# A mixture-of-experts and recurrence kernel: gathered rows as pairs of halves turned by DMA, x mixed before the projections of r and k

## The chip, the cores and the metric

The kernel runs on one core of a Trainium2 chip. Engines: PE (matmuls), DVE, ACT, POOL (here also the issuer of gathers and scatters) and SP (the issuer of all other DMAs). The metric is the device time of one execution in microseconds; the figure for a kernel is the median of its runs.

## The reference

x is 16 x 512 x 128. Its layer norm xn feeds two branches, and the output is x + s * silu(g):

- s is a linear recurrence (16 heads of 8). xx is xn shifted by one token less xn; `xr = xn + xx*maa_r`, `xk = xn + xx*maa_k`, `xv = xn + xx*maa_v`; r, k, v are their projections by 128 x 128 matrices plus a bias; a decayed state runs over the tokens; the result is projected by Wo.
- g is a mixture of experts: a softmax over 8 gates, the two best experts of each token, each expert `(silu(t@w1) * (t@w3)) @ w2` with 512 hidden units, and a shared expert of the same size; half the shared result plus half the weighted sum.

All products are made at nearly full precision: each operand is split in a high and a low half-precision part, and a product is three matmuls (high-high, high-low, low-high).

## The kernel before, in words

**Prologue (0 to some 40 us).** 16 batches of 512 rows are loaded (`rows`), normalised, transposed by PE (`pe_flip`) and kept as `xh` and `xl`, high and low halves with channels on partitions. SP writes the normalised float rows to `normed_rows` in HBM, one write a batch (`sp_normed`, L474), each after the batch's normalisation and independent of the others.

**Steps.** The experts run in 206 steps (`steps`, L310). A unit is 512 rows of the shared expert (16 units), 512 rows sorted for one expert (wide, 25 units) or 256 sorted rows (narrow, 21 units); wide and shared units have four steps, narrow ones two. A step is two up-projections (`pe_up`, L1534, six matmuls of 512 columns), SiLU on ACT (L781), a product on DVE (L1218), a split into halves (ACT L785; DVE L1222 or, in early steps, POOL L624), and, three steps later, the down-projection (`pe_down`, L1561). Steps 0 to 47 are twelve shared units; during them DVE computes the routing, ending in `source` and `dest` (rows to gather, places to scatter to) at step 40. Then come two narrow units, the wide ones and the other narrow ones, with the last four shared units between them.

**Weights.** Nine sets (shared, eight experts) pass through a staging buffer of two slots. SP issues the loads in its program order (`sp_weights`, L459): sets 0 and 1 ahead of the `sp_normed` writes, set k = 2 right behind them, the others in the steps. ACT makes the high half (`act_split_w`, L758, L766), DVE the low one (L1013), in fixed steps: set 2 in steps 8, 10 and 12. ACT, DVE, PE, POOL and SP each work strictly in program order.

**Sorted rows.** There are 71 blocks of 256 sorted rows. POOL (`pool_sorted`, L626) gathers a block by two indirect DMAs of 128 float rows into `srows` (ring of three), and scatters results (`pool_scatter`, L638) by two more; block q's gather stands ahead of block q - 7's scatter, in one fixed order. Before a block is used PE transposes it (`pe_sorted`, L1501, L1509, two transposes), ACT casts the high half (L777) and DVE subtracts for the low one (L1211), into `sx`, a ring of four blocks.

**r and k.** From step 75 on, every fourth step carries one of 32 parts (`part_at`, L418): 512 columns of r (the first 16 parts), then of k (the other 16). The mix with the shifted x is folded into the weights (`wph`, `wpl` hold them scaled by maa and by 1 - maa), so a part is six matmuls, three on x and three on the shifted x (`pe_part`, L1581, L1596). ACT adds the bias (L817), DVE makes the decayed copy (L1232), SP stores both to HBM (`sp_part`, L479). The weights of k, v and Wo are prepared on DVE in steps 72 to 90 (`LATE_STEP`).

**Attention stage.** After the last scatter, 16 units run the recurrence: loads of r, k, their decayed copies and the experts' rows, then matmuls, DVE and POOL work and the output.

SP's order around the change:

```
sp_start()
sp_weights(0)
sp_weights(1)
for b in range(nb):
    sp_normed(b)
k = 2
for i in range(NS):
    while k <= EXPERTS and SPLIT_AT[3 * k - 6] <= i:
        sp_weights(k)
```

Of the kernel before, what the change touches and what calls it, by code (L numbers as in the profile page):

```python
# [12 lines left out]
P = 128  # L13
# [12 lines left out]
UNIT = 256  # L26
# [43 lines left out]
def build(nc, nb, x, decay, per_head, maa, wT, bias, bias_rows, gateT, w1e, w3e, w2e, w1s, w3s, w2s, const, out):  # L70
# [12 lines left out]
    rows_in = nc.dram_tensor("normed_rows", (NTOK, P), F32, kind="Internal").ap()  # L83
# [5 lines left out]
    with ctx:  # L89
# [65 lines left out]
        NXB = 3  # L155
        srows = sb("srows", [P, NXB, TPU, P])
        RING = 4
        sx = sb("sx", [P, 2, RING, UNIT], F16)
        sxh, sxl = [sx[:, i, :, :] for i in range(2)]
# [27 lines left out]
        take = carve(sx[:, :, :, :].rearrange("p a b c -> p (a b c)").bitcast(F32))  # L187
# [33 lines left out]
        ws32r = early([P, 2, P])  # L221
# [6 lines left out]
        ws32 = late([P, 7, P])  # L228
        wph = sb("wph", [P, 7, P], F16)
        wpl = sb("wpl", [P, 7, P], F16)  # L230
# [16 lines left out]
        ypair = take([P, 2, TPU, P])  # L247

# [80 lines left out]
        def flips_at(i):  # L329

            v, j = steps[i]
            todo = blocks_of.get(v + 1, [])
            at = j - (2 if wide(v) else 0) if len(todo) == 1 else j // 2 if wide(v) and j % 2 == 0 else -1 if wide(v) else j
            return [todo[at]] if 0 <= at < len(todo) else []
# [79 lines left out]
        LATE_STEP = 72  # L414
        R_PARTS, PARTS = NA, 2 * NA
# [15 lines left out]
        SCATTER_LAG = 7  # L431

# [7 lines left out]
        def sync_program(e):  # L440
# [12 lines left out]
            def sp_late():  # L453
                nc.sync.wait_ge(sem["normed_out"], 16 * nb)
# [19 lines left out]
            def sp_normed(b):  # L474
                normed(nc.sync, b)
                nc.sync.dma_start(rows_in[b * SEQ:(b + 1) * SEQ, :].rearrange("(t p) d -> p t d", p=P),
                                  rows[:, b * TPS:(b + 1) * TPS, :]).then_inc(sem["normed_out"], 16)

            def sp_part(n):  # L479
                u = n % R_PARTS  # L480
                plain, decayed = (r_rows, rd_rows) if n < R_PARTS else (k_rows, kd_rows)
# [8 lines left out]
            def sp_r(u):  # L490
                if u == 0:
                    nc.sync.wait_ge(sem["w_lo"], 3 * (EXPERTS + 1))
                sp_stored(u)
# [12 lines left out]
            def sp_k(u):  # L506
# [4 lines left out]
                sp_stored(R_PARTS + u)  # L511
# [42 lines left out]
            for b in range(nb):  # L554
                sp_normed(b)
            k = 2
            for i in range(NS):
# [5 lines left out]
                n = part_at(i)  # L563
                if n is not None:
                    sp_part(n)
                if n == RRING + 1:
                    for u in range(RRING - 1):
                        sp_r(u)
                if n == R_PARTS + KRING + 1:
# [34 lines left out]
        def pool_program(e):  # L604
# [21 lines left out]
            def pool_sorted(q):  # L626
                if q == 0:
                    G.wait_ge(sem["normed_out"], 16 * nb)
                    G.wait_ge(sem["source"], 1)
                if q >= NXB:  # L630
                    G.wait_ge(sem["s_flipped"], q - NXB + 1)
                for t in range(TPU):
                    at = block_at[q] * TPU + t
                    G.indirect_dma_start(srows[:, q % NXB, t, :], None, rows_in,  # L634
# [12 lines left out]
            def pool_state0():  # L647
                G.wait_ge(sem["w_hi"], 3 * (EXPERTS + 1))
# [84 lines left out]
        def act_program(e):  # L733
# [24 lines left out]
            def act_split_w(k, part):  # L758
# [3 lines left out]
                if (e, part) == (FREE_EXPERTS, 0):  # L762
                    A.wait_ge(sem["decays"], 4)
                    A.wait_ge(sem["mixes"], 6)
# [7 lines left out]

            def act_sorted(q):
                if q == 0:
                    A.wait_ge(sem["dest"], 1)
                A.wait_ge(sem["s_flipped"], q + 1)
                A.copy(sxh[:, q % RING, :], psum[6][:, q % 2 * UNIT:(q % 2 + 1) * UNIT]).then_inc(sem["s_hi"], 1)  # L777
# [31 lines left out]
            def act_part(n):  # L809
                col = n // R_PARTS  # L810
# [6 lines left out]
                A.activation(rbuf[:, n % 2, :], psum[7], ACT.Identity, bias=brs[:, col:col + 1]).then_inc(sem["part_out"], 1)  # L817

# [81 lines left out]
            for i in range(NS + LAG):  # L900
                y = i - LAG if i >= LAG and last_step_of(i - LAG) else None
                if i < NS:
                    act_up(i)
                    for q in flips_at(i):
                        act_sorted(q)
# [4 lines left out]
                    filled = flips_at(i) or splits_of(i) or block_sets(i - 1)  # L910
                    if y is not None and not filled:
                        act_down(steps[y][0])
                    if part_at(i - 1) is not None:
                        act_part(part_at(i - 1))
                    act_split(i)
                    if y is not None and filled:
# [31 lines left out]
        def dve_program(e):  # L948
# [22 lines left out]
            def dve_r_weights(step):  # L971

                if step == 0:
# [4 lines left out]
                    V.tensor_scalar(ws32r[:, 0, :], w32r[:, :], omx[:, 0:1], SW, ALU.mult, ALU.mult).then_inc(sem["mixes"], 1)  # L978
                    V.tensor_scalar(ws32r[:, 1, :], w32r[:, :], mx[:, 0:1], SW, ALU.mult, ALU.mult).then_inc(sem["mixes"], 1)
                if step == 1:  # L980
                    V.wait_ge(sem["mixes"], 4)
                    V.tensor_copy(wph[:, 0:4:3, :], ws32r[:, :, :]).then_inc(sem["mixes"], 1)
                    V.wait_ge(sem["mixes"], 5)
                    V.tensor_tensor(wpl[:, 0:4:3, :], ws32r[:, :, :], wph[:, 0:4:3, :], ALU.subtract).then_inc(sem["mixes"], 1)
# [70 lines left out]
            def dve_fulls():  # L1055

                V.wait_ge(sem["scanned"], EXPERTS)
                V.wait_ge(sem["normed_out"], 16 * nb)
# [150 lines left out]
            def dve_sorted(q):  # L1209
                V.wait_ge(sem["s_hi"], q + 1)  # L1210
                V.tensor_tensor(sxl[:, q % RING, :], psum[6][:, q % 2 * UNIT:(q % 2 + 1) * UNIT], sxh[:, q % RING, :],  # L1211
                                ALU.subtract).then_inc(sem["s_lo"], 1)

# [10 lines left out]
            def dve_part(n):  # L1224
                w = wb if n < R_PARTS else wk
                V.wait_ge(sem["part_out"], n + 1)
                if n == 0:
                    V.wait_ge(sem["hot_used"], NHOTS)
                    V.wait_ge(sem["mixes"], 7)
# [560 lines left out]
```

## Time and profile before

| | |
|---|---|
| runs | 722.7, 721.18, 720.07 us; median 721.18 us |
| the profiled execution | span 719.3 us from its first to its last instruction; its own device time beside that is not given; the median of the runs is 1.9 us above the span |
| expert stage with sorted rows | first gather 154.67 us, last scatter 554.04 us |
| instructions | 22370; PE 8536 matmuls, DVE 1058, ACT 1008, POOL 519 |

A row of the timeline gives start and duration in us, engine, line, operation, output<-input; in brackets the idle time before it and what ended it. "xN" joins N instructions. The ends of PE's matmuls are modelled, so the pace of PE is read from the distance of starts. A row of the groups of instructions gives shapes, count, busy us and mean ns. DMA issues on SP carry the engine name SPq; landing is from issue to completion.

### The profile page before, as it was taken

The numbers are of one execution on the slowest core, as the hardware profiler recorded it, in microseconds if no ns is written. First come the engines' busy times: TensorE is split into PE (matmuls) and PEld (weight loads), VectorE is DVE, ScalarE is ACT, GpSimd is POOL, SyncE is SP. The second block draws the span as 40 slices with busy tenths as digits, with TensorE's granted clock in tenths as the row PEclk, the third lists the DMA queues.
The fourth block names the chain that finished last, engine by engine and source line by source line (L and its number), as shares of the span: only waits on it lengthen the run. The fifth ranks groups of instructions, "written<-read, shape, count | busy, mean of one in ns | idle before, by whom it ended". The sixth has DMA issues, their size and how long they took to land.

```text
span 719.3 us, 22370 instructions
## 1 busy us (share of the span) xinstructions
PE 654.1 (91%) x8536; PEld 452.1 (63%) x8536; DVE 555.4 (77%) x1058; ACT 494.9 (69%) x1008; POOL 478.9 (67%) x519
## 2 busy tenths in 40 slices
PE   2787897978999999999999999999997899999993
PEld 1544565646665665566666666878886676777772
DVE  5989986877667886667766676667664899999996
ACT  4864798857665656666666666666665788888872
POOL 4844321244777777777777777767778487888873
PEclk9999999999999999999999999999999999999997
DMA  9931111111111323433323334333362767777762
GB/s 243 299 95 45 45 61 46 45 51 36 48 49 49 108 91 108 137 108 108 110 92 109 106 106 139 110 101 108 97 103 93 237 179 230 216 229 222 233 176 59
DMA packets 88616, 86.75 MB, mean 121 GB/s; under 512 B 11394, under 2 KB 65284, under 8 KB 88516
## 3 DMA queue, kind: packets, MB, share of 16 engines
q1 hardware_dynamic: 79428, 66.70, 29.8%
q0 software_dynamic: 9088, 18.63, 9.6%
q8 instruction: 73, 1.20, 0.7%
q14 instruction: 27, 0.22, 0.1%
HBM read 50.82 MB, written 34.47 MB: 119 GB/s over the span
## 4 chain that ended last, share of the span: by engine, by line
PE 53%; DVE 13%; ACT 12%; POOL 11%; issue 7%; DMA 3%; SPq 0%; POOLq 0%; DVEq 0%; ACTq 0%
PE banks L1556 7%; PE banks L1558 7%; PE banks L1557 7%; PE banks L1596 5%; DVE hidden L1218 4%; POOL expert_rows L644 4%; PE banks L1576 4%; PE banks L1577 4%; PE banks L1575 4%; POOL srows L634 3%; ACT hidden L785 3%; PE banks L1621 3%; PE banks L1693 3%; PE banks L1672 3%; ACT rows L823 2%
## 5 line engine op out<-in xcount | busy, mean ns | idle before, releaser
L785 ACT CAST hidden<-hidden 128x512 f16<-128x512 f32 x206 | 127.1, 617 | 135.5 <-DVE hidden L1218 135.4
L634 POOL DMA_INDIRECT srows<-normed_rows,source x142 | 149.7, 1054 | 60.4 <-issue 40.2
L1222 DVE TENSOR_TENSOR hidden<-hidden 128x512 f16<-128x512 f32 x180 | 124.4, 691 | 83.9 <-ACT hidden L785 83.0
L1218 DVE TENSOR_TENSOR hidden<-hidden,banks 128x512 f32<-128x512 f32 x206 | 140.8, 684 | 44.0 <-ACT hidden L781 38.2
L1575 PE MATMUL banks<-wwords,hidden 128*128 (+1 forms) x824 | 148.8, 219 | 1.5 <-DVE hidden L1222 1.1
L1576 PE MATMUL banks<-wwords,hidden 128*128 (+1 forms) x824 | 148.6, 219 | 0.0
L1577 PE MATMUL banks<-wwords,hidden 128*128 (+1 forms) x824 | 148.6, 219 | 0.0
L781 ACT ACTIVATE hidden<-banks 128x512 f32<-128x512 f32 x206 | 122.7, 596 | 28.1 <-PE banks L1558 27.8
L1556 PE MATMUL banks<-sx,wwords 128*128 128x512 f16 (+1 forms) x368 | 121.5, 330 | 3.2 <-DVE wwords L1013 2.7
L1558 PE MATMUL banks<-sx,wwords 128*128 128x512 f16 (+1 forms) x368 | 121.6, 330 | 0.0
L1557 PE MATMUL banks<-sx,wwords 128*128 128x512 f16 (+1 forms) x368 | 121.5, 330 | 0.0
L644 POOL DMA_INDIRECT expert_rows<-ybuf,dest x72 | 77.2, 1072 | 22.8 <-issue 19.8
L1575 PEld LDWEIGHTS banks<-wwords,hidden 128*128 128x128 f16 x824 | 80.6, 98 | 12.4 <-issue 2.0
L644 POOL DMA_INDIRECT expert_rows<-rows,dest x70 | 72.8, 1040 | 23.1 <-issue 20.1
L1576 PEld LDWEIGHTS banks<-wwords,hidden 128*128 128x128 f16 x824 | 80.6, 98 | 11.3
L624 POOL TENSOR_TENSOR hidden<-hidden 128x512 f16<-128x512 f32 x26 | 33.6, 1294 | 76.8 <-ACT hidden L785 76.8
L1303 DVE TENSOR_TENSOR wwords<-banks,wmat 128x1024 f32<-128x1024 f32 x64 | 75.3, 1217 | 10.9 <-PE banks L1672 10.5
L1577 PEld LDWEIGHTS banks<-wwords,hidden 128*128 128x128 f16 x824 | 80.6, 98 | 0.0
L1556 PE MATMUL banks<-xh,wwords 128*128 128x512 f16 x128 | 49.2, 385 | 19.1 <-DVE hidden L1218 18.7
L1321 DVE SCALAR_TENSOR_TENSOR hidden<-banks,cst,hidden 128x256 f32<-128x256 f32 x128 | 61.5, 481 | 3.8 <-ACT hidden L849 0.7
L1558 PEld LDWEIGHTS banks<-sx,wwords 128*128 x368 | 36.0, 98 | 25.6
L1557 PE MATMUL banks<-xl,wwords 128*128 128x512 f16 x128 | 49.0, 383 | 0.0
(218 smaller groups left out, 1429.7 us busy)
## 6 DMA issues: line engine op xcount, KB each, us to landing
rows<-x SPq DMA_DIRECT2D x32, 256.0 KB, 4.9
rows<-expert_rows SPq DMA_DIRECT2D x32, 256.0 KB, 3.6
normed_rows<-rows SPq DMA_DIRECT2D x16, 256.0 KB, 3.9
r_rows<-rows SPq DMA_DIRECT2D x16, 256.0 KB, 2.1
rd_rows<-rows SPq DMA_DIRECT2D x16, 256.0 KB, 2.2
stage<-r_rows SPq DMA_DIRECT2D x16, 256.0 KB, 4.0
k_rows<-rows SPq DMA_DIRECT2D x16, 256.0 KB, 2.2
kd_rows<-rows SPq DMA_DIRECT2D x16, 256.0 KB, 2.2
```

The costliest lines, as they stand in the source:

```text
L634: G.indirect_dma_start(srows[:, q % NXB, t, :], None, rows_in, bass.IndirectOffsetOnAxis(source[:, at:at + 1], 0)).then_inc(sem[f"s_in{q % ...
L644: G.indirect_dma_start(rows_out, bass.IndirectOffsetOnAxis(dest[:, at:at + 1], 0), ring_of(q)[:, t, :], None).then_inc(sem[f"y_stored{q % ...
L781: A.activation(sg[:, i % 2, :], psum[2 * (i % 2)][:, :], ACT.Silu, scale=1.0 / SW).then_inc(sem["silu"], 1)
L785: A.copy(guh[:, i % 4, :], gu[:, i % 2, :]).then_inc(sem["gu_hi"], 1)
L1218: V.tensor_tensor(gu[:, i % 2, :], sg[:, i % 2, :], psum[2 * (i % 2) + 1][:, :], ALU.mult).then_inc(sem["gated"], 1)
L1222: V.tensor_tensor(gul[:, i % 4, :], gu[:, i % 2, :], guh[:, i % 4, :], ALU.subtract).then_inc(sem["gu_lo"], 1)
L1556: T.matmul(o, a, mh, start=True, stop=False)
L1557: T.matmul(o, a, ml, start=False, stop=False)
L1558: k = T.matmul(o, b, mh, start=False, stop=True)
L1575: T.matmul(o, guh[:, i % 4, s], a, start=(j == 0 and n == 0), stop=False)
L1576: T.matmul(o, guh[:, i % 4, s], b, start=False, stop=False)
L1577: k = T.matmul(o, gul[:, i % 4, s], a, start=False, stop=last)
```

## The change

1. Rows for the gather are kept as pairs: `normed_rows` holds, per token, 128 high and 128 low halves (512 bytes as before). SP makes them by transposing `xh` and `xl` batch by batch with DMA transposes (two a batch, 128 x 512 halves each) into a buffer with two slots, and writes each slot out.
2. A gathered block is turned by one DMA transpose on SP (`sp_turn`) straight into `sx`; PE's transposes, ACT's cast and DVE's subtraction for blocks go. `srows` becomes a ring of five. SP's turns stand in its program order at the first step of the unit before.
3. r and k take turns (part n is r for even n, k for odd n). x is mixed ahead: sum of the halves (DVE, one in two parts, four steps ahead), scaled shifted part (ACT, four steps ahead), mix (DVE, three ahead), high half (ACT, two ahead), low half (DVE, two ahead); a part is then three matmuls. The stores follow three steps after.
4. Weights of k, v and Wo are prepared from step 50 on; r and k weights are no longer scaled by maa.

```diff
+        NXB = 5
+        srows = sb("srows", [P, NXB, TPU, 2, P], F16)
+        PAIRS = NXB * TPU // TPS
...
-            def sp_normed(b):
-                normed(nc.sync, b)
+            def sp_pair(b):
+                s = b % PAIRS
+                nc.sync.wait_ge(sem["x_lo"], b + 1)
+                if b >= PAIRS:
+                    nc.sync.wait_ge(sem[f"pair_out{s}"], 16 * (b // PAIRS))
+                for h, half in enumerate((xh, xl)):
+                    nc.sync.dma_start(pairs[:, s, :, h, :], half[:, b * XS + 2:(b + 1) * XS],
+                                      transpose=True).then_inc(sem[f"pair_in{s}"], 16)
+
+            def sp_pair_out(b):
+                s = b % PAIRS
+                nc.sync.wait_ge(sem[f"pair_in{s}"], 32 * (b // PAIRS + 1))
                 nc.sync.dma_start(rows_in[b * SEQ:(b + 1) * SEQ, :].rearrange("(t p) d -> p t d", p=P),
-                                  rows[:, b * TPS:(b + 1) * TPS, :]).then_inc(sem["normed_out"], 16)
+                                  pairs[:, s, :, :, :].rearrange("p t h d -> p t (h d)")).then_inc(sem[f"pair_out{s}"], 16)
+
+            def sp_turn(q):
+                nc.sync.wait_ge(sem[f"s_in{q % NXB}"], 16 * TPU * (q // NXB + 1))
+                if q >= RING:
+                    nc.sync.wait_ge(sem["up"], last_up[unit_of[q - RING]])
+                nc.sync.dma_start(sx[:, q % RING, :, :, :].rearrange("p t h d -> p (t h) d"),
+                                  srows[:, q % NXB, :, :, :].rearrange("p t h d -> p (t h d)"),
+                                  transpose=True).then_inc(sem[f"turned{q % RING}"], 16)
...
-            for b in range(nb):
-                sp_normed(b)
+            for b in range(nb + 1):
+                if b < nb:
+                    sp_pair(b)
+                if b >= 1:
+                    sp_pair_out(b - 1)
...
+                for q in turned_at(i):
+                    sp_turn(q)
+                n = part_at(i - 3)
...
                 if q >= NXB:
-                    G.wait_ge(sem["s_flipped"], q - NXB + 1)
+                    turned(G, q - NXB)
...
+            def dve_mix(n):
+                proj = n % 2
+                V.wait_ge(sem["mix_prev"], n + 1)
+                m = mixed[:, :].rearrange("p (b i) -> p b i", b=4)
+                V.scalar_tensor_tensor(m, xsum[:, :, 1:P + 1], omx[:, proj:proj + 1], m, ALU.mult, ALU.add).then_inc(sem["mixed"], 1)
...
             def pe_part(n):
+                T.matmul(psum[7], wph[:, proj, :], mix_hi[:, :], start=True, stop=False)
+                T.matmul(psum[7], wph[:, proj, :], mix_lo[:, :], start=False, stop=False)
+                T.matmul(psum[7], wpl[:, proj, :], mix_hi[:, :], start=False, stop=True).then_inc(sem["part"], 1)
```

## Rows read from the trace of the kernel before

**Rows 1.** The page, part 1: busy us, share of the span, instructions.
```profile
PE 654.1 (91%) x8536; PEld 452.1 (63%) x8536; DVE 555.4 (77%) x1058; ACT 494.9 (69%) x1008; POOL 478.9 (67%) x519
```

**Rows 2.** Windows of 50 us: PE, PEld, DVE, ACT, POOL busy (count), clock, DMA.
```profile
335.00:385.00 50.00, 50.00 (x432) 31.69 (x431) 34.40 (x57) 32.40 (x62) 37.86 (x38) 1.00 0.32 106
385.00:435.00 50.00, 50.00 (x431) 31.68 (x429) 35.22 (x58) 32.18 (x62) 38.16 (x37) 1.00 0.31 103
```

**Rows 3.** Waits of POOL, 185 to 556 us: total us, times, longest.
```profile
POOL expert_rows L644 <- issue: 39.9, 131, 0.3
POOL srows L634 <- issue: 36.9, 121, 0.3
POOL srows L634 <- PE banks L1509: 4.7, 5, 3.5
```

**Rows 4.** Timeline of POOL: first gather, third block's scatter, last scatter.
```profile
154.67 1.36 POOL L634 DMA_INDIRECT srows<-normed_rows,source  x1 [5.73 <-DVE source L1174]
...
197.52 0.99 POOL L644 DMA_INDIRECT expert_rows<-rows,dest  x1 [1.18 <-ACT rows L805]
...
554.04 0.97 POOL L644 DMA_INDIRECT expert_rows<-rows,dest  x1 [0.31 <-issue]
```

**Rows 5.** Timeline of PE, 350 to 361 us: one wide unit.
```profile
350.66 0.38 PE L1556 MATMUL banks<-sx,wwords 128*128 128x512 f16 x1
...
351.95 0.38 PE L1509 MATMUL banks<-cst,srows 128*128 128x128 f32 x2
352.17 0.22 PE L1575 MATMUL banks<-wwords,hidden 128*128 x1
...
358.95 0.38 PE L1596 MATMUL banks<-xh,wph 128*128 128x512 f16 x1
...
360.27 0.38 PE L1556 MATMUL banks<-sx,wwords 128*128 128x512 f16 x1
```

**Rows 6.** Timeline of SP, 14 to 62 us: issues and their durations.
```profile
16.23 0.83 SPq L472 DMA_DIRECT2D stage<-w1s  x1
17.10 1.61 SPq L472 DMA_DIRECT2D stage<-w3s  x1
...
22.50 16.44 SPq L476 DMA_DIRECT2D normed_rows<-rows  x16
39.12 0.70 SPq L472 DMA_DIRECT2D stage<-w1e  x1
39.87 0.44 SPq L472 DMA_DIRECT2D stage<-w3e  x1
```

**Rows 7.** Groups of instructions: shapes, count, busy us, mean ns.
```profile
L1222 DVE TENSOR_TENSOR hidden<-hidden 128x512 f16<-128x512 f32 x180 | 124.4, 691 | 83.9 <-ACT hidden L785 83.0
...
L857 ACT ACTIVATE wwords<-stage,cst 128x512 f32<-128x512 f32 x64 | 42.3, 713 | 0.0
...
L1211 DVE TENSOR_TENSOR sx<-banks,sx 128x256 f16<-128x256 f32 x71 | 29.6, 417 | 1.5 <-ACT sx L777 1.5
...
L777 ACT CAST sx<-banks 128x256 f16<-128x256 f32 x71 | 26.0, 367 | 3.1 <-PE banks L1509 3.1
```

**Rows 8.** Timeline of ACT and DVE at step 8: the third set's first split.
```profile
63.26 0.62 ACT L766 ACTIVATE wwords<-stage 128x512 f16<-128x512 f32 x1
...
66.55 0.68 DVE L1013 SCALAR_TENSOR_TENSOR wwords<-stage,wwords 128x512 f16<-128x512 f32 x1
```

**Rows 9.** DMA issues: count, KB each, median us from issue to landing.
```profile
rows<-x SPq DMA_DIRECT2D x32, 256.0 KB, 4.9
...
normed_rows<-rows SPq DMA_DIRECT2D x16, 256.0 KB, 3.9
r_rows<-rows SPq DMA_DIRECT2D x16, 256.0 KB, 2.1
...
out<-rows SPq DMA_DIRECT2D x15, 256.0 KB, 2.7
...
stage<-w2e SPq DMA_DIRECT2D x8, 256.0 KB, 3.8
```

More of the change, by code:

```diff
@@ L227, in build @@
         w32 = late([P, 4, P])
-        ws32 = late([P, 7, P])
-        wph = sb("wph", [P, 7, P], F16)
-        wpl = sb("wpl", [P, 7, P], F16)
+        ws32 = late([P, 5, P])
+        wph = sb("wph", [P, 5, P], F16)
+        wpl = sb("wpl", [P, 5, P], F16)
+        xsum = sb("xsum", [P, 4, P + 1])
         brk = sb("brk", [P, 2])
@@ L247, in build @@
         ypair = take([P, 2, TPU, P])
+        take = carve(stage[:, :, :].rearrange("p a b -> p (a b)"))
+        mixed = take([P, 512])
+        mix_hi, mix_lo = [take([P, 512], F16) for i in range(2)]
         def ring_of(q):
@@ L327, in last_step_of, with turned_at @@
             return i + 1 == NS or first_step(i + 1)
-        def flips_at(i):
+        def turned_at(i):
             v, j = steps[i]
-            todo = blocks_of.get(v + 1, [])
-            at = j - (2 if wide(v) else 0) if len(todo) == 1 else j // 2 if wide(v) and j % 2 == 0 else -1 if wide(v) else j
-            return [todo[at]] if 0 <= at < len(todo) else []
+            return blocks_of.get(v + 1, []) if j == 0 else []
+        last_up = {v: i + 1 for i, (v, j) in enumerate(steps)}
         def where(u):
@@ L431, in build, with pairs_out, turned @@
         SCATTER_LAG = 7
+        def pairs_out(engine):
+            for s in range(PAIRS):
+                engine.wait_ge(sem[f"pair_out{s}"], 16 * len(range(s, nb, PAIRS)))
+        def turned(engine, q):
+            engine.wait_ge(sem[f"turned{q % RING}"], 16 * (q // RING + 1))
         def low_done(engine, i):
@@ L647, in pool_state0 @@
             def pool_state0():
+                G.wait_ge(sem["part"], PARTS)
                 G.wait_ge(sem["w_hi"], 3 * (EXPERTS + 1))
@@ L817, in act_part, with act_previous, act_mix_high @@
                 A.activation(rbuf[:, n % 2, :], psum[7], ACT.Identity, bias=brs[:, col:col + 1]).then_inc(sem["part_out"], 1)
+            def act_previous(n):
+                u, proj = divmod(n, 2)
+                A.wait_ge(sem["xsum"], u + 1)
+                if n == 0:
+                    A.wait_ge(sem["w_lo"], 3 * (EXPERTS + 1))
+                    A.wait_ge(sem["mix_in"], 48)
+                else:
+                    A.wait_ge(sem["mix_lo"], n)
+                A.mul(mixed[:, :].rearrange("p (b i) -> p b i", b=4), xsum[:, :, 0:P], mx[:, proj:proj + 1]).then_inc(sem["mix_prev"], 1)
+            def act_mix_high(n):
+                A.wait_ge(sem["mixed"], n + 1)
+                if n >= 1:
+                    A.wait_ge(sem["part"], n)
+                A.copy(mix_hi[:, :], mixed[:, :]).then_inc(sem["mix_hi"], 1)
             def act_tokens(m):
@@ L1234, in dve_part, with dve_xsum, dve_mix_low @@
                                 rep_mid(w[:, :], WIDE // Q), ALU.mult).then_inc(sem["part_decayed"], 1)
+            def dve_xsum(u):
+                tt, g = where(u)
+                if u == 0:
+                    V.wait_ge(sem["x_lo"], nb)
+                    V.wait_ge(sem["zero_cols"], 2 * nb)
+                h, l = [a[:, 4 * g * XS:4 * (g + 1) * XS].rearrange("p (b s) -> p b s", s=XS)[:, :, 1 + tt * P:2 + (tt + 1) * P]
+                        for a in (xh, xl)]
+                V.tensor_tensor(xsum[:, :, :], h, l, ALU.add).then_inc(sem["xsum"], 1)
+            def dve_mix(n):
+                proj = n % 2
+                V.wait_ge(sem["mix_prev"], n + 1)
+                if n == 0:
+                    V.wait_ge(sem["mixes"], 1)
+                m = mixed[:, :].rearrange("p (b i) -> p b i", b=4)
+                V.scalar_tensor_tensor(m, xsum[:, :, 1:P + 1], omx[:, proj:proj + 1], m, ALU.mult, ALU.add).then_inc(sem["mixed"], 1)
+            def dve_mix_low(n):
+                V.wait_ge(sem["mix_hi"], n + 1)
+                if n >= 1:
+                    V.wait_ge(sem["part"], n)
+                V.tensor_tensor(mix_lo[:, :], mixed[:, :], mix_hi[:, :], ALU.subtract).then_inc(sem["mix_lo"], 1)
             def dve_masks(step):
@@ L1407, in dve_program @@
                     dve_split(i)
-                if part_at(i - 2) is not None:
-                    dve_part(part_at(i - 2))
+                if part_at(i + 4) is not None and part_at(i + 4) % 2 == 0:
+                    dve_xsum(part_at(i + 4) // 2)
+                if part_at(i + 3) is not None:
+                    dve_mix(part_at(i + 3))
+                if part_at(i + 2) is not None:
+                    dve_mix_low(part_at(i + 2))
+                if part_at(i - 3) is not None:
+                    dve_part(part_at(i - 3))
                 if i < 5:
@@ L1543, in pe_up @@
                     if j == 0:
-                        T.wait_ge(sem["s_lo"], blocks[-1] + 1)
+                        for q in blocks:
+                            turned(T, q)
                     q = blocks[0] % RING
-                    mh, ml = [a[:, q:q + len(blocks), :].rearrange("p b i -> p (b i)") for a in (sxh, sxl)]
+                    mh, ml = [sx[:, q:q + len(blocks), :, h, :].rearrange("p q t d -> p (q t) d") for h in range(2)]
                 else:
```

145 lines of the change are left out of this document (56 added, 89 removed).

## The prediction, made before the changed kernel was run

> **What bounds the kernel now.** The page's busy shares come first [rows 1]: PE 91%, POOL 67%, and the reader is tempted to call the kernel PE-bound, with room on POOL. The windows of the expert stage agree at first sight [rows 2]: in 50 us PE is busy for all 50, and POOL for 38, with 38 indirect DMAs of about 1.0 us. The waits of POOL between 185 and 556 us [rows 3] fill the rest: 131 waits before scatters and 121 before gathers, together 76.8 us, end in "issue", at 0.3 us each, the gap that every indirect DMA has behind the one before it. The largest wait on another engine is 4.7 us, on PE's transposes; the rest are smaller, on the copies into the scatter buffers. So POOL runs back to back. From the third block's scatter at 197.52 us to the end of the last at 555.01 us [rows 4] it issues 260 indirect DMAs (284 in all, less 20 gathers and four scatters before), 1.375 us each, four to a block of 256 rows: 5.50 us for a block, 11.0 us for a wide unit of two blocks. PE needs 360.27 - 350.66 = 9.61 us for the same wide unit [rows 5]. PE is full because four shared units are mixed in, which cost POOL nothing; over the whole stage the two have about equal work, and POOL's ends last, with a scatter at 554.04 us. The attention stage waits for them and runs the same instructions in both kernels.
>
> The first 48 steps (shared expert, routing) are another regime: one chain through ACT and DVE, with PE and POOL waiting, and SP bringing each expert's weights ahead. There the view to read is SP's timeline [rows 6]: sixteen write-outs of normalised rows from 22.50 us, all in flight together, and at 39.12 us the loads of the third weight set (k = 2).
>
> **The change, part by part.**
>
> Matmuls of r and k: three of six go, 32 times. Six take 360.27 - 358.95 = 1.32 us, so 0.66 us x 32 = 21.1 us of PE [rows 5]. The transposes of gathered rows go: a pair takes 352.17 - 351.95 = 0.22 us [rows 5], x 71 = 15.6 us. PE loses 36.7 us of work, in a stage that POOL paces; a wide unit falls to about 9.61 - 0.66 - 0.44 = 8.5 us against POOL's 11.0. POOL keeps all 284 indirect DMAs, of the same bytes. I cost the saving at nothing for the time. If POOL's pace were not the bound, it would be up to 36.7 us (a rival below).
>
> ACT and DVE: per block ACT loses a 0.37 us cast and DVE a 0.42 us subtraction. Per part ACT gains a scaling (nearest 0.71 us) and a cast (taken the same), DVE a mix and a low part (nearest 0.69 us each) and half a sum (0.35 us) [rows 7]. Over a wide unit with one part that is +0.7 us on ACT and +0.9 us on DVE. They are busy 32 and 34 us of 50 [rows 2], so this lies in idle time, as do the ten weight-preparation steps that DVE now does 22 steps earlier. Without that cover it would be 32 x 0.9 = 29 us.
>
> Gather ring of five instead of three, released by the transpose DMA: POOL's waits on PE's transposes go, 4.7 us less five gaps of 0.3 = 3.2 us, and as much again at most with the smaller waits, 6 us [rows 3]. POOL's order is fixed, though: the scatter at 197.52 us waits for the first wide unit's output, which now comes only a few 0.22 us earlier. I take 2 us, between 0 and 6.
>
> Turns inside the expert stage: 71 DMA transposes on SP, each behind the gather and ahead of the unit's first matmul. SP waits there for a gather, and stores of r and k stand behind; their buffers are double and a part comes once in four steps. A turn has most of a unit's 11 us. Cost nothing, as long as one takes under 5.5 us; cover and limit are both POOL's block period.
>
> **The prologue is what costs.** SP no longer issues sixteen independent writes. For each of 16 batches it issues two transposes, then waits for the previous batch's pair to land, writes that pair out, and, with two slots, may not issue the next two transposes before that write has landed. Everything behind is held: SP's next item is the third weight set, which ACT splits in step 8 at 63.26 us and DVE at 66.55 us [rows 8]. ACT and DVE are in order, so when those weights are late, all of routing and the first gather (154.67 us [rows 4]) move by as much.
>
> Let I be SP's time to issue one transpose and L the landing time of a 256 KB write. One batch takes P = L + 2I. The first write-out goes at 22.5 + 4I, the fifteenth 14P later; 2 us for the last pair to land, 0.4 us for its write-out's issue, 0.8 us for two load issues, 3.8 us for the third load to land [rows 9], 0.6 us for ACT's split. Against DVE's 66.55 us the delay is D = 4I + 14P - 36.45 us (22.5 + 2 + 0.4 + 0.8 + 3.8 + 0.6 = 30.1; 30.1 - 66.55 = -36.45).
>
> L: the same write lands in 3.9 us with fifteen others beside it, a 256 KB write of 512-byte rows to the output in 2.7 us, one of 2 KB rows in 2.1 us [rows 9]. I take 2.7: same pieces, few others in flight. I: no transpose is in the trace. A plain issue takes 0.44 us, those of w1s and w3s, which go in 256-byte pieces, 0.83 and 1.61 us [rows 6]. A row of a 128x128 block of halves is 256 bytes too, so I take the mean of these two, 1.2 us; 0.4 and 1.6 are the ends. Then P = 2.7 + 2.4 = 5.1 and D = 4.8 + 71.4 - 36.45 = 39.8 us. Low: I = 0.4, P = 3.5, D = 14.2. Lowest: L = 2.1, P = 2.9, D = 5.8. High: I = 1.6, L = 3.9, P = 7.1, D = 69.4.
>
> The Trainium skill has a rule that speaks for the low end: Advanced Engine Details and Errata, X-Bar Transpose (TRN2), says that transpose DMAs are as fast as regular ones. By it I would be a plain issue and the time about 733 us. No run here shows it.
>
> Sum: the profiled execution spans 719.3 us; 719.3 + 39.8 - 2 = 757.1. The median of the three runs, 721.18 us, lies 1.9 us above that span, so 759 us.
>
> **Rivals.**
>
> (A) Not slower: the loop is short enough. Place: SP between 22.5 and 60 us. Point: 4I + 14P under 36.45, that is P under about 2.5 us; then no weights are late and POOL's 4 us of waits are left as a gain: 719.3 - 4 + 1.9 = 717 us. For it: ACT does not want that set before 63 us [rows 8]. Against it: the shortest landing of such a write, 2.1 us, alone nearly fills P.
>
> (B) PE's saving counts. Place: 197 to 545 us. If POOL's 5.50 us per block were stretched by waiting rather than its own, the stage would follow PE: 759 + 2 - 36.7 = 724 us with the stall, 699 us with the stall at its low end. For it: PE at 50 of 50 us. Against it: POOL's waits on others, of which the largest kind sums to 4.7 us in 370 [rows 3].
>
> (C) Transposes are slow on the DMA engines themselves. If one takes as long as a 256 KB load of x, 4.9 us [rows 9], two per batch follow one another: P = 9.8, the first write-out at 32.3, the sixteenth at 179.3, weights split at 184.9, D = 118: 719.3 + 118 + 1.9 = 839 us. The expert stage still holds, as 4.9 is under 5.5 us per block; above that it would lengthen by 71 times the excess. For it: 2-byte elements cross all partitions. Against it: 128 KB is half of such a load, and no HBM is involved.
> The Trainium skill prices it: VectorE: DVE Perf Modes, The three transpose paths, gives 1309 ns for one 128x128 by DMA; four of them, as an estimate 5.2 us, would make it about 850 us. No row here shows the like.
>
> **How the numbers follow.** A measurement here tells some 0.3% (2 us) from no change. Forecast (stall of 14 to 70 us, no gain from PE): 78%. A: 8%, nearly all faster by over 0.3%. B: 6%, of which a third faster, the rest near or above. C: 8%. So faster 0.09, same 0.03, slower 0.88. The forecast's own range is 719.3 + 14.2 - 6 + 1.9 = 729 to 719.3 + 69.4 + 1.9 = 791; the lowest D gives 721 to 727 and (C) lies above. I give 725 to 800, leaving out A and most of C.
>
> **What would show it.** SP's write-outs of pairs spaced by about 5 us from 27 to 100 us, where sixteen stood in 16.4 us; the loads of the third set near 100 us instead of 39.12; ACT's split of it ended by a DMA, with PE, DVE and POOL idle for some 40 us; the first gather near 194 us; from there POOL again in gaps of 0.30 us, the last scatter about 400 us after the first gather as before, PE busy some 80% of the stage with gaps that end in DMA; the attention stage as long as now. Wrong it would be if the pairs' write-outs come every 2.5 us, if POOL's period per block falls below 5.3 us, or if the first matmul of units waits on turns while gathers have long landed.

## The result, and the profile after

The changed kernel takes 809.68 us (807.82 to 810.11) against 720.62 us of the kernel before, run beside it: a ratio of 1.121 [1.118, 1.123]. Slower, as forecast, but by 89 us where 38 were forecast, and 9.7 us above the range. The profiled execution spans 807.6 us, 88.3 more than before. Of the six executions of run 9 below, one took 3606.76 us; the figures given for that run are those of the other five. The first view is POOL's timeline, which cuts the span in three.

```profile
198.28 1.33 POOL L670 DMA_INDIRECT srows<-normed_rows,source  x1 [5.77 <-DVE source L1222]
...
640.07 0.97 POOL L680 DMA_INDIRECT expert_rows<-rows,dest  x1 [0.30 <-issue]
```

Against [rows 4] the first gather is 43.6 us later (198.28 - 154.67). From the first gather to the end of the last scatter, the "stage" of all that follows, 442.76 us pass where it was 400.34: 42.4 more. The attention stage behind it grew by 2.3 (166.6 from 164.3). So there are two losses of nearly the same size, and only one of them was forecast.

**The first loss, ahead of the stage.** SP's timeline answers to [rows 6].

```profile
22.36 1.31 SPq L493 DMA_TRANSPOSE srows<-xh  x1
...
29.22 0.39 SPq L499 DMA_DIRECT2D normed_rows<-srows  x1
...
50.40 0.58 SPq L499 DMA_DIRECT2D normed_rows<-srows  x1
52.95 1.20 SPq L493 DMA_TRANSPOSE srows<-xh  x1
54.19 1.27 SPq L493 DMA_TRANSPOSE srows<-xl  x1
55.51 0.58 SPq L499 DMA_DIRECT2D normed_rows<-srows  x1
...
102.09 1.56 SPq L499 DMA_DIRECT2D normed_rows<-srows  x2
103.69 0.54 SPq L485 DMA_DIRECT2D stage<-w1e  x1
```

Most transposes hold SP for 1.20 to 1.27 us, and a batch takes 5.11 us (from 50.40 to 55.51, as in most of the loop). SP stands idle between a write-out's issue (ends at 50.98) and the next transpose (52.95): it waits for a slot. The third weight set is asked for at 103.69 instead of 39.12. The page's DMA issues, after, give the landing times (count, KB each, median us):

```profile
normed_rows<-srows SPq DMA_DIRECT2D x16, 256.0 KB, 2.5
...
srows<-xh SPq DMA_TRANSPOSE x16, 2.4
srows<-xl SPq DMA_TRANSPOSE x16, 2.5
```

ACT's and DVE's timelines, after, show who pays [rows 8]:

```profile
108.48 0.63 ACT L803 ACTIVATE wwords<-stage 128x512 f16<-128x512 f32 x1 [45.03 <-DMA stage<-w2e]
...
109.15 0.69 DVE L1061 SCALAR_TENSOR_TENSOR wwords<-stage,wwords 128x512 f16<-128x512 f32 x1 [43.23 <-ACT wwords L803]
```

DVE's split of the third set comes 42.6 us later than before (109.15 for 66.55).

**The second loss, in the stage.** The windows, after (PE, PEld, DVE, ACT, POOL busy, clock, DMA), answer to [rows 2]:

```profile
355.00:405.00 50.00, 39.98 (x334) 23.26 (x333) 33.20 (x52) 31.11 (x55) 29.30 (x29) 1.00 0.45 123
405.00:455.00 50.00, 42.02 (x345) 24.18 (x344) 34.16 (x53) 30.64 (x56) 36.52 (x36) 1.00 0.40 110
```

PE has fallen to about 41 us of 50, which was expected, but POOL has fallen too, to 29 in the first window: it is no longer the bound. No engine is near full, and DVE and ACT are about as busy as before. POOL's timeline, after, says what it waits for:

```profile
406.36 1.00 POOL L680 DMA_INDIRECT expert_rows<-rows,dest  x1 [1.67 <-ACT rows L836]
...
428.36 1.00 POOL L680 DMA_INDIRECT expert_rows<-rows,dest  x1 [1.03 <-ACT rows L836]
...
450.37 1.00 POOL L680 DMA_INDIRECT expert_rows<-rows,dest  x1 [1.03 <-ACT rows L836]
...
482.63 1.00 POOL L680 DMA_INDIRECT expert_rows<-rows,dest  x1 [11.30 <-ACT rows L836]
```

Two wide units take 22.0 us (from 406.36 to 428.36, and again to 450.37), which POOL nearly matches (it waits 1.03 us), and a shared unit between them costs 11.3 us that POOL spends waiting. A step lasts 2.75 us in the mean, whichever unit it belongs to: eight steps in 22.0 us, which makes 11 for the four of a shared unit. The waits of ACT between 198 and 620 us, after (total us, times, longest), point at DVE:

```profile
ACT hidden L816 <- DVE hidden L1261: 107.4, 118, 3.8
ACT stage L864 <- DVE stage L1294: 29.7, 32, 1.0
ACT stage L858 <- DVE xsum L1286: 21.9, 16, 1.4
```

and DVE's timeline, after, shows what is done in a step:

```profile
405.14 0.69 DVE L1265 TENSOR_TENSOR hidden<-hidden 128x512 f16<-128x512 f32 x1 [0.68 <-ACT hidden L816]
405.75 0.69 DVE L1300 TENSOR_TENSOR stage<-stage 128x512 f16<-128x512 f32 x1
406.35 0.68 DVE L1261 TENSOR_TENSOR hidden<-hidden,banks 128x512 f32<-128x512 f32 x1
407.72 0.69 DVE L1265 TENSOR_TENSOR hidden<-hidden 128x512 f16<-128x512 f32 x1 [0.68 <-ACT hidden L816]
408.33 0.69 DVE L1275 TENSOR_TENSOR rows<-rows,wk 128x512 f32<-128x512 f32 x1
408.93 0.68 DVE L1261 TENSOR_TENSOR hidden<-hidden,banks 128x512 f32<-128x512 f32 x1
```

The product (L1261) is cast by ACT (L816), DVE subtracts that cast (L1265), then comes one instruction that belongs to r and k (here the low half of the mixed x, then the decay), and only then the next step's product. So DVE waits 0.68 us for ACT in each step, and ACT waits for DVE's product in each step: a loop through two engines that work in order, 2.58 us from 406.35 to 408.93, in which each is idle for part of the time. The step with the sum of x is longer still (3.93 us, from the product at 397.20 to that at 401.13), since ACT's scaling behind its cast waits 1.4 us for that sum.

**Theory T**: the second loss is this loop. Each instruction of the mix that stands between DVE's split and the next product lengthens a step by its own 0.60 us (408.33 to 408.93). **The rival R**: the turns on SP, or the gather path, hold the stage.

### The profile page after: what moved, and what is told of

It is laid out like the page before. It is cut to its first block, busy times and chain, and to the rows that moved or that the text cites. A ratio compares the mean times of both kernels' runs of the same rounds, so it can differ in the third digit from the quotient of the medians.

```text
span 807.6 us, 22114 instructions
## 1 busy us (share of the span) xinstructions
PE 640.2 (79%) x8298; PEld 427.3 (53%) x8298; DVE 576.6 (71%) x1063; ACT 508.1 (63%) x1001; POOL 470.1 (58%) x519
## 4 chain that ended last, share of the span: by engine, by line
DVE 28%; ACT 25%; issue 16%; PE 14%; DMA 7%; SPq 4%; POOL 3%; DVEq 0%; ACTq 0%; POOLq 0%
ACT hidden L816 12%; DVE hidden L1261 11%; SPq L493 4%; DMA normed_rows<-srows 4%; ACT hidden L812 3%; DVE stage L1294 3%; PE banks L1748 3%; DVE rows L1275 3%; DVE stage L1300 3%; PE banks L1728 3%; PE banks L1677 2%; ACT stage L864 2%; ACT rows L870 2%; ACT stage L858 2%; POOL hidden L707 1%
## 5 line engine op out<-in xcount | busy, mean ns | idle before, releaser
L816 ACT CAST hidden<-hidden 128x512 f16<-128x512 f32 x206 | 127.1, 617 | 136.0 <-DVE hidden L1261 134.4
L1265 DVE TENSOR_TENSOR hidden<-hidden 128x512 f16<-128x512 f32 x180 | 124.7, 693 | 106.1 <-ACT hidden L816 103.7
L1261 DVE TENSOR_TENSOR hidden<-hidden,banks 128x512 f32<-128x512 f32 x206 | 140.4, 682 | 47.0 <-ACT hidden L812 46.4
L670 POOL DMA_INDIRECT srows<-normed_rows,source x142 | 142.6, 1004 | 51.9 <-issue 42.7
L1618 PE MATMUL banks<-sx,wwords 128*128 128x512 f16 (+1 forms) x368 | 123.6, 336 | 59.2 <-DVE hidden L1261 46.1
L1637 PE MATMUL banks<-wwords,hidden 128*128 (+1 forms) x824 | 151.5, 220 | 4.1 <-issue 3.0
L1638 PE MATMUL banks<-wwords,hidden 128*128 (+1 forms) x824 | 150.6, 220 | 0.0
L1639 PE MATMUL banks<-wwords,hidden 128*128 (+1 forms) x824 | 150.3, 220 | 0.0
L1620 PE MATMUL banks<-sx,wwords 128*128 128x512 f16 (+1 forms) x368 | 122.8, 334 | 0.0
L1619 PE MATMUL banks<-sx,wwords 128*128 128x512 f16 (+1 forms) x368 | 122.8, 334 | 0.0
L1618 PEld LDWEIGHTS banks<-xh,wwords 128*128 128x128 f16 x128 | 12.4, 97 | 81.1 <-DVE hidden L1261 72.7
```

The costliest lines, as they stand in the source:

```text
L670: G.indirect_dma_start(srows[:, q % NXB, t, :, :].rearrange("p h d -> p (h d)"), None, rows_in, bass.IndirectOffsetOnAxis(source[:, at:at ...
L816: A.copy(guh[:, i % 4, :], gu[:, i % 2, :]).then_inc(sem["gu_hi"], 1)
L1261: V.tensor_tensor(gu[:, i % 2, :], sg[:, i % 2, :], psum[2 * (i % 2) + 1][:, :], ALU.mult).then_inc(sem["gated"], 1)
L1265: V.tensor_tensor(gul[:, i % 4, :], gu[:, i % 2, :], guh[:, i % 4, :], ALU.subtract).then_inc(sem["gu_lo"], 1)
L1618: T.matmul(o, a, mh, start=True, stop=False)
L1619: T.matmul(o, a, ml, start=False, stop=False)
```

## The experiments

Ratios are to the kernel before, run on the same chip.

### 1. Weights between the pairs

```diff
                 if b >= 1:
                     sp_pair_out(b - 1)
+                if b in (4, 8, 12):
+                    sp_weights(b // 4 + 1)
-            k = 2
+            k = 5
```

> Edit: the loads of the third, fourth and fifth weight set are issued between the pairs (behind the fifth, ninth and thirteenth batch's pair) instead of behind all sixteen. Theory T (SP's loop of pairs holds the weights, and that is worth about 44 us; the expert stage's 43 us is another matter): ACT's wait for the third set, 45.0 us, goes; the first gather comes at 155 to 160 us instead of 198.28, unless the pairs' own end (about 105 to 110 us) binds, which it does not, since the first gather needs them only behind routing; the expert stage stays at about 443 us; time 764 to 768 us. Rival R (routing or the first gather is gated by the pairs or by something else than the weights): first gather at 180 us or later, time 790 us or more.

Measured: 766.61 us, 1.064 [1.059, 1.069]. ACT's wait for the third set is gone, and the first gather is here (POOL's timeline of this run):

```profile
156.74 1.33 POOL L672 DMA_INDIRECT srows<-normed_rows,source  x1 [5.76 <-DVE source L1224]
```

The stage is 442.0 us. The pairs take as long as ever (the last write-outs go at 105.67 us), but nothing needs them until the first gather. The first loss is what SP holds back, not the pairs themselves: 43.1 us.

### 2. Six matmuls, no mix

```diff
-                    if part_at(i + 2) is not None:
-                        act_mix_high(part_at(i + 2))
                     act_split(i)
-                    if part_at(i + 4) is not None:
-                        act_previous(part_at(i + 4))
...
-                if part_at(i + 4) is not None and part_at(i + 4) % 2 == 0:
-                    dve_xsum(part_at(i + 4) // 2)
-                if part_at(i + 3) is not None:
-                    dve_mix(part_at(i + 3))
-                if part_at(i + 2) is not None:
-                    dve_mix_low(part_at(i + 2))
```

with the folded weights and the six matmuls of the kernel before.

> Edit: x is not mixed ahead; the parts of r and k are six matmuls on folded weights again, on the same steps as in the changed kernel; pairs, gathers and turns by DMA stay as changed. Theory T (the mix lies inside the loop of ACT and DVE that a step's length is made of): from first gather to the end of the last scatter about 400 to 410 us instead of 442.8, in spite of 21 us more of matmuls; first gather still at about 198 us; time 765 to 775 us. Rival R (the turns on SP, or POOL waiting for them, lengthen the stage): stage stays at 435 to 445 us or grows, time 800 to 815 us.

Measured: 761.04 us, 1.053 [1.048, 1.059]; the stage is 390.5 us, as POOL's timeline of this run shows:

```profile
201.31 1.33 POOL L665 DMA_INDIRECT srows<-normed_rows,source  x1 [5.76 <-DVE source L1198]
...
590.79 0.97 POOL L675 DMA_INDIRECT expert_rows<-rows,dest  x1 [0.30 <-issue]
```

R falls: the turns are all there and the stage is 10 us shorter than in the kernel before. It is also shorter than T had said, because T had no gain in it for the gather path.

### 3. The gather path of before, with the mix

```diff
-            for b in range(nb + 1):
-                if b < nb:
-                    sp_pair(b)
-                if b >= 1:
-                    sp_pair_out(b - 1)
+            for b in range(nb):
+                sp_normed(b)
...
-                for q in turned_at(i):
-                    sp_turn(q)
```

with float rows, PE's transposes, ACT's cast, DVE's subtraction and the ring of three as before.

> Edit: the gather path of the kernel before (float rows, sixteen write-outs without waits between them, transposes on PE, halves by ACT and DVE), with x mixed ahead as in the changed kernel. Theory T: no stall on weights, first gather at 152 to 160 us; the expert stage as long as in the changed kernel or longer, 443 to 460 us, since the mix is in it and the flips' copies and subtractions come on top; time 760 to 785 us. Rival R (the turns cost the expert stage its 43 us): stage 400 us or less, time 700 to 725 us.

Measured: 764.85 us, 1.060 [1.056, 1.064]; first gather at 155.34, stage 441.6 us. The mix alone brings the second loss, with no DMA transpose in the kernel.

### 4. The same instructions in another order

```diff
-                    act_split(i)
                     if part_at(i + 4) is not None:
                         act_previous(part_at(i + 4))
+                    act_split(i)
...
-                if not low_on_pool(i):
-                    dve_split(i)
-                if part_at(i + 4) is not None and part_at(i + 4) % 2 == 0:
-                    dve_xsum(part_at(i + 4) // 2)
                 if part_at(i + 3) is not None:
                     dve_mix(part_at(i + 3))
                 if part_at(i + 2) is not None:
                     dve_mix_low(part_at(i + 2))
                 if part_at(i - 3) is not None:
                     dve_part(part_at(i - 3))
+                if not low_on_pool(i):
+                    dve_split(i)
+                if part_at(i + 5) is not None and part_at(i + 5) % 2 == 0:
+                    dve_xsum(part_at(i + 5) // 2)
```

The sum of x also moves a step ahead, from `i + 4` to `i + 5`.

> Edit: nothing but the places of the mix's instructions in ACT's and DVE's order: ACT scales the next part ahead of its split of the hidden values instead of behind it, DVE mixes, makes the low half and scales the part's decay ahead of its split, and sums x a step earlier, behind its split. The same instructions on every engine. Theory T (the places of the mix in the loop from ACT's activation over DVE's product to ACT's split lengthen a step from 2.0 to 2.75 us): the expert stage falls to 400 to 415 us of 442.8, time 768 to 782 us. Rival R1 (the plain sum of work on ACT and DVE, or the turns, sets the step, wherever the instructions stand): stage 435 to 445 us, time 800 to 812 us.

Measured: 754.99 us, 1.047 [1.043, 1.052]; stage 387.6 us, shorter than T's range. POOL's timeline of this run:

```profile
199.25 1.33 POOL L670 DMA_INDIRECT srows<-normed_rows,source  x1 [5.76 <-DVE source L1222]
...
585.93 0.97 POOL L680 DMA_INDIRECT expert_rows<-rows,dest  x1 [0.31 <-issue]
```

DVE's timeline of this run:

```profile
397.20 0.67 DVE L1261 TENSOR_TENSOR hidden<-hidden,banks 128x512 f32<-128x512 f32 x1
397.79 0.68 DVE L1300 TENSOR_TENSOR stage<-stage 128x512 f16<-128x512 f32 x1
398.55 0.69 DVE L1265 TENSOR_TENSOR hidden<-hidden 128x512 f16<-128x512 f32 x1
399.16 0.68 DVE L1261 TENSOR_TENSOR hidden<-hidden,banks 128x512 f32<-128x512 f32 x1
399.76 0.69 DVE L1275 TENSOR_TENSOR rows<-rows,wk 128x512 f32<-128x512 f32 x1
400.53 0.69 DVE L1265 TENSOR_TENSOR hidden<-hidden 128x512 f16<-128x512 f32 x1
401.14 0.68 DVE L1261 TENSOR_TENSOR hidden<-hidden,banks 128x512 f32<-128x512 f32 x1
```

The low half (L1300) and the decay (L1275) stand between the product and the split, where DVE had been waiting for ACT's cast; these two steps take 1.96 and 1.98 us, and the waits of 0.68 us are filled. Not one instruction was saved, and the whole second loss is gone. POOL's DMAs follow one another in gaps of 0.30 us again, nearly all of them.

### 5. and 6. How much for one instruction, how much for three

Of the changed kernel, only the low half is moved ahead of the split:

```diff
+                if part_at(i + 2) is not None:
+                    dve_mix_low(part_at(i + 2))
                 if not low_on_pool(i):
                     dve_split(i)
...
-                if part_at(i + 2) is not None:
-                    dve_mix_low(part_at(i + 2))
```

> Edit of the changed kernel: one instruction per part, DVE's subtraction that makes the low half of the mixed x, stands ahead of DVE's split of the hidden values instead of behind it. Theory T (each instruction of DVE that stands between its split and the next product lengthens that step by its own 0.60 us, since the split waits for ACT's cast, that for the product, and the product stands behind it): 32 x 0.60 = 19 us off the stage's 442.8, so 420 to 427 us, time 787 to 794 us. Rival (it is ACT's two waits for DVE's sum and mix, 1.36 and 0.92 us, that lengthen a step; the low half is not in them): stage 438 to 443 us, time 805 to 810 us.

Measured: 790.44 us, 1.093 [1.089, 1.097]; the stage (200.07 to 622.83) is 422.8 us, 20.0 us shorter. Meanwhile ACT's two waits for the sum and the mix are as long as in the changed kernel, as this run's waits of ACT show (total us, times, longest):

```profile
ACT stage L864 <- DVE stage L1294: 29.8, 32, 1.0
ACT stage L858 <- DVE xsum L1286: 21.9, 16, 1.4
```

Then DVE's mix, low half and decay ahead of the split, ACT untouched:

```diff
                 if part_at(i + 3) is not None:
                     dve_mix(part_at(i + 3))
...
                 if part_at(i - 3) is not None:
                     dve_part(part_at(i - 3))
+                if not low_on_pool(i):
+                    dve_split(i)
```

> Edit of the changed kernel: DVE's mix, low half and decay stand ahead of its split; its sum of x, and ACT's scaling, stay behind the splits. Theory T: 96 x 0.60 = 58 us off 442.8 would be 385 us, which is under what POOL's DMAs need (387.6 us with all moved), so the stage stops there: 388 to 398 us, time 755 to 764 us. Rival (ACT's scaling behind its split, and its wait for the sum, still lengthen one step in four so that they bind): 405 us or more, time 771 us or more.

Measured: 759.21 us, 1.054 [1.050, 1.058]; the stage is 391.3 us (198.69 to 589.94). The loop can be priced by the instruction, 0.60 us times 32, until POOL's own pace takes over. ACT's scaling and its wait for the sum (21.9 us here too) no longer hold the stage.

### 7. Four slots for pairs

```diff
-        PAIRS = NXB * TPU // TPS
...
+        PAIRS = 4
+        pairs = [a[:, i * (TPS // TPU):(i + 1) * (TPS // TPU), :, :, :].rearrange("p q t h d -> p (q t) h d")
+                 for a in (srows, sx) for i in range(2)]
```

> Edit: four slots for pairs instead of two (two more in the buffer of turned rows, unused by then), so that SP need not wait for a write-out before the next but one pair. Nothing else of the changed kernel is edited. Theory T (a batch takes the landing of a write plus two issues, L + 2I = 5.11 us, because of the slots; without that wait it takes what SP's three issues take, 2 x 1.24 + 0.4 to 0.6 = 2.9 to 3.1 us): the third set's loads go at 70 to 75 us instead of 103.69, ACT's wait for it is 12 to 17 us instead of 45.0, time 776 to 782 us. Rival (the DMA engines carry one transpose at a time, 2.4 us each, or transposes and write-outs queue behind one another): a batch still takes 4.5 us or more, time 800 us or more.

Measured: 785.82 us, 1.086 [1.082, 1.089]. SP's timeline of this run:

```profile
44.51 1.21 SPq L494 DMA_TRANSPOSE sx<-xh  x1
45.77 1.27 SPq L494 DMA_TRANSPOSE sx<-xl  x1
47.08 0.58 SPq L500 DMA_DIRECT2D normed_rows<-srows  x1
47.76 1.21 SPq L494 DMA_TRANSPOSE sx<-xh  x1
...
79.51 0.54 SPq L486 DMA_DIRECT2D stage<-w1e  x1
```

A batch takes 3.25 us, SP's own issues back to back, and the third set is asked for 24.2 us earlier; ACT's wait for it is 19.5 us, the time 23.9 us less than the changed kernel's. All a little more than expected (a few transposes hold SP for 2 to 2.9 us), but the form L + 2I holds: the landing of the write-out goes away with the slots, the issues stay. The edit also makes DVE wait for the last write-outs before it uses the borrowed buffer; the first gather comes 24.2 us earlier (174.10), as much as the loads, so no cost of that wait shows.

### 8. to 10. The parts recombined

Weights between the pairs and the new order, both:

```diff
+                if b in (4, 8, 12):
+                    sp_weights(b // 4 + 1)
...
                     if part_at(i + 4) is not None:
                         act_previous(part_at(i + 4))
+                    act_split(i)
```

> Edit: both of the earlier edits that helped, weights issued between the pairs and the mix's instructions in other places of ACT's and DVE's order. Theory T (two separate losses, one ahead of the expert stage and one in it, that add): 809.7 less 43.1 less 54.7 = 712 us, between 708 and 717, under the kernel before by 0.5 to 2%; first gather at about 157 us, stage about 388 us. Rival (the two losses cover each other in part, or POOL's first scatters hold the stage's start): 720 us or more.

Measured: 709.88 us, 0.983 [0.980, 0.986]: the two losses add, and without them the change beats the kernel before, by 13.3 us or 1.7%. First gather at 154.91, stage 384.1 us.

The same without the mix (edits 1 and 2 together):

```diff
+                if b in (4, 8, 12):
+                    sp_weights(b // 4 + 1)
...
-                    if part_at(i + 2) is not None:
-                        act_mix_high(part_at(i + 2))
```

> Edit: weights issued between the pairs, and six matmuls without the mix; what is left of the change is the gathers of pairs turned by DMA, the ring of five, and the pairs' write-out. Theory T (the gather path alone is worth the 10 us by which the stage of the run with six matmuls, 390.5 us, is shorter than before, 400.3; POOL no longer waits for PE's transposes): 761.0 less 43.1 = 718 us, 713 to 722. If the mix's three matmuls saved are worth PE's 21 us, this one is 20 us slower than the run with both edits; if POOL paces the stage, it is within 6 us of it.

Measured: 716.06 us, 0.990 [0.988, 0.993]; stage 389.5 us. So the gather path by DMA is worth about 7 us by itself, and the mix, put where DVE waits, another 5 to 6.

The mix in the new order on the gather path of before (edits 3 and 4 together):

```diff
+            for b in range(nb):
+                sp_normed(b)
...
                     if part_at(i + 4) is not None:
                         act_previous(part_at(i + 4))
+                    act_split(i)
```

> Edit: gather path of the kernel before, x mixed ahead in the other order on ACT and DVE: the mix alone, without its harm. Theory T (POOL paces the stage, so 21 us of matmuls saved are worth nothing): stage 395 to 405 us, time 714 to 726 us, as the kernel before. Rival B of the prediction (PE's saving counts): 705 us or less. If the flips' copies and subtractions on top of the mix fill the loop of ACT and DVE again: 730 us or more.

Measured: 727.91 us, 1.008 [1.005, 1.011], between T's range and the third case of the expectation (730 us or more); stage 402.7 us. The mix alone gains nothing here, it loses 4.7 us. So the two parts of the change do not simply add: 7.1 us gained by the gather path alone and 4.7 lost by the mix alone, but 13.3 gained by both. On this path POOL paces the stage and its indirect DMAs take longer in the mean. The groups of POOL, 230 to 530 us, of this run and, behind it, of the one with both edits (count, busy us, mean ns, idle time):

```profile
L639 POOL DMA_INDIRECT srows<-normed_rows,source x108 | 114.7, 1062 | 33.3 <-issue 31.4 <-PE banks L1565 1.9
L649 POOL DMA_INDIRECT expert_rows<-ybuf,dest x56 | 61.0, 1090 | 17.1 <-issue 16.1 <-ACT rows L811 0.3 <-ACT rows L813 0.3
```

```profile
L672 POOL DMA_INDIRECT srows<-normed_rows,source x110 | 111.7, 1015 | 33.5 <-issue 33.5
...
L682 POOL DMA_INDIRECT expert_rows<-ybuf,dest x58 | 59.2, 1020 | 17.7 <-issue 17.4 <-ACT rows L838 0.3
```

## Why the prediction was right, and where it failed

**The prologue: right in mechanism and nearly in size.** I = 1.2 was taken and 1.20 to 1.27 measured, L = 2.7 taken and 2.5 measured, P = 5.1 taken and 5.11 measured; the loads go at 103.69 us, where the working gives 101. The stall on the first gather is 43.6 us, 39.8 forecast: the first write-out was late by 2 us (29.22 for 27.3), a few of the transposes held SP for 2 us instead of 1.27, and from DVE's split to the first gather pass 89.1 us instead of 88.1. Run 1 shows that the stall is worth 43 us, run 7 that P consists of what was said. That I was met so closely is in part luck: it was the mean of two unlike plain issues, 0.83 and 1.61 us, and no run shows that their 256-byte pieces are what makes a transpose's issue long. One reading behind L was off: the sixteen write-outs of the kernel before were not all in flight together. They went out over 16.4 us and landed in 3.9 each, so some four were in flight at a time (an estimate from these two numbers).

The Trainium skill's rule for the low end (Advanced Engine Details and Errata, X-Bar Transpose (TRN2): transposes as fast as regular DMAs) does not hold for SP's issues here: a transpose holds it for 1.20 to 1.27 us, a plain write-out for 0.58 in the same stretch. The Trainium skill's price behind rival C (VectorE: DVE Perf Modes, The three transpose paths: 1309 ns for one 128x128 by DMA) does not carry over to four in one DMA, which the prediction estimated from it at 5.2 us: a 128x512 transpose landed in 2.4 us.

**The expert stage: wrong, and this is the step that failed.** "They are busy 32 and 34 us of 50 [rows 2], so this lies in idle time": the mix was put at nothing in the sum. The idle time of ACT and DVE was not free time: each waited for the other, once a step, and an instruction put between the split and the next product does not use that idle time but moves it. The text even priced the loss of cover, "32 x 0.9 = 29 us", and did not put it into the sum; it is also too little, since the work on ACT and DVE is not what counts but the place of each instruction. By the stages, the mix in the order of the change costs 442.8 - 390.5 = 52.3 us, 1.6 us a part, although PE has three matmuls less in each; in the other order it costs nothing (387.6). The view that would have shown it is DVE's timeline of the kernel before, which the prediction did not use. [rows 7] already held a sign: of the 83.9 us that DVE is idle ahead of its splits (L1222), 83.0 end in ACT's cast. ACT's group on the page of the kernel before is the other half of the loop, and DVE's timeline shows that there, too, the split of a step waits for ACT's cast of the product just before it:

```profile
L785 ACT CAST hidden<-hidden 128x512 f16<-128x512 f32 x206 | 127.1, 617 | 135.5 <-DVE hidden L1218 135.4
...
356.34 0.69 DVE L1222 TENSOR_TENSOR hidden<-hidden 128x512 f16<-128x512 f32 x1 [0.68 <-ACT hidden L785]
356.95 0.68 DVE L1232 TENSOR_TENSOR rows<-rows,wb 128x512 f32<-128x512 f32 x1
357.55 0.68 DVE L1218 TENSOR_TENSOR hidden<-hidden,banks 128x512 f32<-128x512 f32 x1
```

and the decay behind the split already held up the next product, one step in four.

**POOL as the bound: right, and lost.** POOL paced the stage before and paces it in runs 2, 4, 6 and 8 to 10; in the changed kernel it waits for ACT's copies out. The prediction's own sign of being wrong (a period under 5.3 us) did not come; the waits on copies, 11.3 us at a shared unit, did. The clause "four shared units are mixed in, which cost POOL nothing" no longer holds when a step takes 2.75 us.

**The ring: its gain taken too small.** Taken as 2 us, between 0 and 6; for the whole gather path it is, by stages, 400.3 - 390.5 = 9.8 us, by the times of run 9 about 7. Most of it is not the waits for PE's transposes (4.7 us [rows 3]): from the third block's scatter to the end the 260 DMAs take 349.0 us in run 2 against 357.5, 1.342 us each instead of 1.375, that is 8.5 us.

**Rival B (PE's saving counts): a quarter of the matmuls at most.** Between runs 9 and 8, 21 us of matmuls go and the stage falls by 5.4 us; on the gather path of before none of it shows (402.7 us in run 10 for 400.3). PE's transposes, 15.6 us, go together with the rest of the gather path, and no run parts them from its 9.8 us. Rivals A and C did not come: P was neither under 2.5 nor near 9.8 us.

**The sum again**, on the profiled span: 719.3 + 43.6 (39.8 forecast) + 42.4 (-2 forecast) + 2.3 = 807.6 us.

## What to carry to other kernels

Two engines that hand a value back and forth once a step, in order, form a loop whose length is a bound of its own, and their idle time inside it is not room. Before adding work to them, write out one step from the timeline and ask of every new instruction whether it stands where the engine waits for the other (then it is free) or between what it has just received and what the other waits for (then it costs its full length in every step). And a queue that issues in order makes everything behind a slow loop late: what is needed first goes ahead of it, or into its gaps.

## What had not been expected of the hardware

- A DMA transpose of 128x512 halves (128 KB) landed in 2.4 to 2.5 us, in the time that a write of 256 KB took (2.5), and held SP twice as long as that write's issue (1.20 to 1.27 us for 0.58).
- While the kernel stalled from 62 to 107 us, PE was busy for 4.3 of 45 us and its granted clock was 0.60 in the mean (between its two levels, 1.2 and 2.4 GHz), then 0.77 until 125 us. It cost 1.0 us at most: from DVE's split of the third set to the first gather pass 89.1 us (109.15 to 198.28), where it was 88.1 (66.55 to 154.67). The windows, after:

```profile
62.00:107.00 45.00, 4.28 (x36) 2.50 (x36) 3.78 (x11) 1.12 (x2) 1.16 (x1) 0.60 0.46 115
107.00:125.00 18.00, 11.31 (x83) 6.49 (x84) 15.66 (x26) 9.23 (x17) 6.58 (x5) 0.77 0.23 75
```

- Where POOL runs back to back, its gathers take 1.06 us in the mean on the path of before (run 10) and 1.02 on the new one (run 8), with the same bytes, and the scatters differ likewise (1.09 and 1.02). The medians of a gather in the kernel before and in the changed one are both 0.99 us, so it is some long ones that go. No run tells why, and this stays open. Over 142 gathers and 142 scatters these means make some 17 us (an estimate), most of the 18.6 us between the stages of runs 10 and 8.
